# A relational graph layer: key one-hots by 16-bit pairs, source one-hots in three comparisons, additions set between other work

## The reference

```python
def _L0_gnn_ref(feat, weight, src, dst, etypes):
    h_src = feat[src]
    msg = jnp.zeros((h_src.shape[0], weight.shape[2]), dtype=feat.dtype)
    for r in range(num_rels):
        mask = etypes == r
        msg = msg + h_src * mask[:, None].astype(feat.dtype) @ weight[r]
    return jax.ops.segment_sum(msg, dst, num_segments=feat.shape[0])
h = jnp.maximum(_layernorm(x, axis=-1), 0.0)
x = x + _L0_gnn_ref(h, L0_gnn_weight, src, dst, edge_type_16)
```

## Time and profile before

| | |
|---|---|
| median of three | 1113.21 us |
| the profiled execution | 1110.19 us |
| its span, first to last instruction | 1108.4 us |
| TensorE (PE) busy | 958.2 us, 86% |
| VectorE (DVE) busy | 910.3 us, 82% |
| GpSimd (POOL) busy | 807.5 us, 73% |
| ScalarE (ACT) busy | 530.7 us, 48% |
| granted TensorE clock, mean | 0.966 |

### The profile page before, as it was taken

One profiled execution on the slowest core, in us unless ns is written; L12 is line 12 of the kernel. 1 busy time (PEld: TensorE's weight loads), 2 busy tenths in 40 slices (PEclk: granted clock), 3 DMA queues, 4 the chain that ended last, 5 costly groups with the idle time before them and its releaser, 6 DMA issues.

```text
span 1108.4 us, 57958 instructions
## 1 busy us (share of the span) xinstructions
PE 958.2 (86%) x24205; PEld 809.6 (73%) x24205; DVE 910.3 (82%) x3137; ACT 530.7 (48%) x1548; POOL 807.5 (73%) x644
## 2 busy tenths in 40 slices
PE   3999988899988888988899888989799798888996
PEld 1445777788877777877788777778687687776885
DVE  7755889898888689887899887998788689886884
ACT  4886454454445345544444453544344345444441
POOL 3231888888888888888787887878888888887760
PEclk9998999999999899998999998999999999998998
DMA  6697322222322222222232222232222222221312
GB/s 183 259 391 287 81 69 63 64 64 75 82 65 66 63 64 65 64 66 64 67 85 66 65 63 66 63 85 67 64 66 64 64 65 65 68 82 45 87 44 61
DMA packets 42713, 98.10 MB, mean 89 GB/s; under 512 B 14749, under 2 KB 14751, under 8 KB 42452
## 3 DMA queue, kind: packets, MB, share of 16 engines
q1 hardware_dynamic: 14870, 45.60, 12.3%
q0 software_dynamic: 19616, 20.13, 10.7%
q10 hardware_dynamic: 7966, 28.64, 6.7%
HBM read 66.69 MB, written 27.62 MB: 85 GB/s over the span
## 4 chain that ended last, share of the span: by engine, by line
PE 42%; DVE 26%; issue 12%; ACT 7%; POOL 7%; DMA 5%; DVEq 2%; ACTq 1%; POOLq 0%
PE ps L1288 15%; PE ps L1305 13%; DVE u L964 9%; POOL u L532 6%; DVE u L954 4%; PE ps L1329 4%; ACT u L605 3%; DMA u<-table,row_idx 3%; PE ps L1343 3%; DVE spreadv L872 2%; DVE accT L980 2%; ACT u L691 2%; DMA table<-u 2%; DVE rank L834 2%; PE ps L1210 1%
## 5 line engine op out<-in xcount | busy, mean ns | idle before, releaser
L532 POOL DMA_INDIRECT u<-table,row_idx x575 | 740.8, 1288 | 210.7 <-issue 140.5
L674 ACT CAST u<-ps 128x384 bf16<-128x384 f32 (+1 forms) x684 | 294.5, 465 | 443.5 <-PE ps L1288 433.3
L1288 PE MATMUL ps<-parts,u 128*128 128x192 bf16 x3724 | 356.2, 250 | 0.7 <-ACT key_p L595 0.5
L1288 PEld LDWEIGHTS ps<-parts,u 128*128 128x128 bf16 x3724 | 308.8, 99 | 11.5 <-issue 7.8
L1305 PE MATMUL ps<-u 32*64 32x272 bf16 (+1 forms) x15808 | 297.2, 279 | 8.4 <-issue 8.2
L964 DVE TENSOR_SCALAR u<-iota_key,z_sb 128x272 bf16<-128x272 f16 x1292 | 280.9, 286 | 8.8 <-DVE win_x L862 6.9
L1305 PEld LDWEIGHTS ps<-u 32*64 32x64 bf16 x15808 | 227.4, 105 | 49.7 <-issue 31.8
L954 DVE TENSOR_SCALAR u<-u,node_id 128x1152 bf16<-128x1152 f16 (+1 forms) x456 | 197.0, 487 | 0.0
L691 ACT COPY u<-ps 128x272 f32<-128x272 f32 (+3 forms) x304 | 102.0, 421 | 60.8 <-PE ps L1305 60.8
L980 DVE TENSOR_TENSOR accT<-accT,u 128x17 f32 (+1 forms) x392 | 71.3, 182 | 65.0 <-DVE accT L980 26.2
L1329 PE MATMUL ps<-u,w_cat 128*64 128x136 f32 x1216 | 90.4, 289 | 6.7 <-issue 5.2
(11 more groups left out here) (134 smaller groups left out, 769.9 us busy)
## 6 DMA issues: line engine op xcount, KB each, us to landing
u<-rel_dram SPq DMA_DIRECT2D x76, 544.0 KB
table<-u ACTq DMA_DIRECT2D x24, 1024.0 KB, 5.2
u<-table,row_idx POOLq DMA_INDIRECT x575
rel_dram<-rel_row SPq DMA_DIRECT2D x76, 4.2 KB
x_sb<-x SPq DMA_DIRECT2D x2, 448.0 KB
out<-h_sb SPq DMA_DIRECT2D x3, 224.0 KB
out<-h_sb ACTq DMA_DIRECT2D x3, 224.0 KB
msg_x<-table,spill_row POOLq DMA_INDIRECT x38
```

The lines of the kernel that those rows point to most:

```text
L532: pool.indirect_dma_start(out=msg_p[:, b, j, :], out_offset=None, in_=table, in_offset=bass.IndirectOffsetOnAxis(ap=row_idx[:, j, m:m + 1] ...
L674: act.copy(msg_s[:, u % MB, 0:width, :].rearrange("p q c -> p (q c)"), ps[gather_bank(u)][:, 0:width * ROW]).then_inc(s_gev, 1)
L1288: last = pe.matmul(there, hot[:, part % HRING, t - q * SK, at * P:(at + 1) * P], parts[:, t, :], start=t == blocks[0], stop=t == blocks[-1])
```

## The change

- **Key one-hots.** `z_sb` becomes 16-bit, and ACT writes each value twice, side by side. `key_hots` now makes a whole chunk, 6, 6 or 5 ranges, in one comparison of two tensors, `iota_key` against the pairs: 1632, 1632 or 1360 elements instead of 272. The ring `khot` has six chunks (two pairs of supers) as before.
- **Source one-hots.** Three comparisons for the whole pair (2176, 2048 and 2048 elements) instead of six. The ring `hot` has two whole pairs instead of three halves.
- **Slots and spills.** `placed` compares tensors of 16-bit pairs as well, for which the ranks are copied to pairs first (`rank2`). Spilled edges are ranked, placed and permuted once per two pairs ("two quads" of targets) instead of once per pair. `sort_turn` is a 16-bit matmul. All sorting steps use 128 partitions instead of 104, so GpSimd's prologue fills the other rows of `vals`.
- **Order.** `add_sums` is a generator, and the main loop of VectorE takes one addition from it after each of its larger steps. On TensorE the permutation goes from the end of chunk 0 to the middle of chunk 1, the turn from chunk 1 to chunk 2, and the batches of gathered rows are all summed in chunk 1. The planner's model has new costs for these.

```diff
-    KR, HCH, GB, MB = 34, ((0, 9), (9, SQ)), -(-SQ // 2), 9
-    HPART, HRING = max(high - low for low, high in HCH), 3
+    KR, HRING, GB, MB = 6, 2, -(-SQ // 2), 9
...
-    sum_at = (1, 1, 2, 2)
+    sum_at = (1, 1, 1, 1)
     def sort_pair(n, c, ahead, at):
         return n + ahead if n + ahead < NPR and c == at else None
-    permuted = lambda n, c: sort_pair(n, c, 2, 0)
-    turned = lambda n, c: sort_pair(n, c, 2, 1)
-    spilled = lambda n, c: sort_pair(n, c, 2, 2)
+    permuted = lambda n, c: sort_pair(n, c, 2, 1)
+    turned = lambda n, c: sort_pair(n, c, 2, 2)
     ranked = lambda n, c: sort_pair(n, c, 3, 2)
+    def spill_ranked(n, c):
+        return (n + 1) // 2 if c == 2 and n % 2 == 1 and n + 2 < NPR else None
+    def spill_placed(n, c):
+        return n // 2 if c == 0 and n % 2 == 0 else None
...
+            pool.tensor_copy(ident16[:, :], ident[:, :]).then_inc(s_const, 1)
+            pool.memset(z_sb[:, :, :], 0.0).then_inc(s_const, 1)
+            pool.wait_ge(s_const, 12)
+            pool.memset(vals[96:P, :, :, :], -1.0).then_inc(s_const, 1)
+            pool.wait_ge(s_const, 13)
             pool.memset(vals[:, :, 0:HJ, 4:5], 0.0).then_inc(s_const, 1)
             pool.memset(vals[:, :, HJ:SJ, 4:5], float(SW)).then_inc(s_const, 1)
-            pool.wait_ge(s_const, 10)
+            pool.wait_ge(s_const, 15)
...
-            def placed(hots, a, j, first, ranks, n):
-                there = hots[0:TP, :, :].rearrange("p j (a z) -> p a j z", a=a)
-                places = iota_slot[0:TP, first:first + n].rearrange("p (a j z) -> p a j z", a=1, j=1).to_broadcast([TP, a, j, n])
-                mine = ranks.rearrange("p (a j z) -> p a j z", j=j, z=1).to_broadcast([TP, a, j, n])
+            def placed(hots, first, ranks, tiles, n):
+                there = hots.rearrange("p t (h o) -> p t h o", o=2)
+                places = iota_slot[:, first:first + n].rearrange("p (t h o) -> p t h o", t=1, o=2).to_broadcast([P, tiles, n // 2, 2])
+                mine = ranks.rearrange("p t (h o) -> p t h o", h=1).to_broadcast([P, tiles, n // 2, 2])
                 return dve.tensor_tensor(there, places, mine, ALU.is_equal)
             def sort_slots(g):
                 dve.wait_ge(s_ranked, g + 1)
                 dve.wait_ge(s_ranges, g + 1)
-                step(dve.tensor_tensor(ranks[0:TP, :, :], ps[6][0:TP, 0:PT * SQ].rearrange("p (c q) -> p c q", q=SQ), ranges[0:TP, :, :],
-                                       ALU.mult))
-                step(dve.tensor_reduce(rank[0:TP, :], ranks[0:TP, :, :], AX, ALU.add))
+                dve.tensor_tensor(ranks[:, :, :], ps[6][:, 0:PT * SQ].rearrange("p (c q) -> p c q", q=SQ), ranges[:, :, :],
+                                  ALU.mult).then_inc(s_rread, 1)
+                dve.wait_ge(s_rread, g + 1)
+                step(dve.tensor_reduce(rank[:, :], ranks[:, :, :], AX, ALU.add))
+                by_tile = rank[:, :].rearrange("p (a j o) -> p a j o", j=HJ, o=1).to_broadcast([P, WINS, HJ, 2])
+                step(dve.tensor_copy(rank2[:, :, :].rearrange("p (j a) o -> p a j o", a=WINS), by_tile))
                 if g >= 1:
                     dve.wait_ge(s_z, g)
-                    dve.wait_ge(s_srank, g)
-                placed(slot_hot, WINS, HJ, 0, rank[0:TP, :], CAP).then_inc(s_slots, 1)
-                dve.tensor_scalar(spill_mask[0:TP, :], rank[0:TP, :], float(CAP), None, ALU.is_ge).then_inc(s_mask, 1)
+                placed(slot_hot, 0, rank2[:, :, :], PT, CAP).then_inc(s_slots, 1)
+                if g >= 2:
+                    dve.wait_ge(s_srank, g // 2)
+                dve.tensor_scalar(spill_mask[:, g % 2, :], rank[:, :], float(CAP), None, ALU.is_ge).then_inc(s_mask, 1)
...
-            def source_hots(n, c):
-                b, part, (low, high) = n % BCR, len(HCH) * n + c, HCH[c]
-                dve.wait_ge(s_bc[b], 16 * (n // BCR + 1))
-                if part >= HRING:
-                    last_n, last_c = divmod(part - HRING, len(HCH))
-                    dve.wait_ge(s_gat, GB * last_n + -(-HCH[last_c][1] // 2))
-                for k in range(SK):
-                    there = min(high, (NT - k + SK - 1) // SK)
-                    last = dve.tensor_scalar(hot[:, part % HRING, k, 0:(there - low) * P], bc[:, b, low * P:there * P],
-                                             node_id[:, k:k + 1], None, ALU.is_equal)
-                last.then_inc(s_hot, 1)
-            def key_hots(n, low, high):
+            def source_hots(n, k):
+                there = min(SQ, (NT - k + SK - 1) // SK)
+                if k == 0:
+                    dve.wait_ge(s_bc[n % BCR], 16 * (n // BCR + 1))
+                    if n >= HRING:
+                        dve.wait_ge(s_gat, GB * (n - HRING + 1))
+                last = dve.tensor_scalar(hot[:, n % HRING, k, 0:there * P], bc[:, n % BCR, 0:there * P], node_id[:, k:k + 1], None,
+                                         ALU.is_equal)
+                if k == SK - 1:
+                    last.then_inc(s_hot, 1)
+            def key_hots(n, c):
+                own, part = ranges_of(n, c), n * len(CHUNKS) + c
                 dve.wait_ge(s_zev, WINS * (n + 1))
-                for q in range(low, high):
-                    v = n * SQ + q
-                    if v >= KR:
-                        dve.wait_ge(s_agg, v - KR + 1)
-                    dve.tensor_scalar(khot[:, v % KR, :], iota_key[:, :], z_sb[:, n % 3, 1, q:q + 1], None, ALU.is_equal).then_inc(s_khot, 1)
+                if part >= KR:
+                    dve.wait_ge(s_agg, (n - KR // len(CHUNKS)) * SQ + own[-1] + 1)
+                there = khot[:, part % KR, 0:len(own), :].rearrange("p q (h o) -> p q h o", o=2)
+                keys = iota_key[:, :].rearrange("p (q h o) -> p q h o", q=1, o=2).to_broadcast([P, len(own), KEYS // 2, 2])
+                mine = z_sb[:, n % 3, 2 * (SQ + own[0]):2 * (SQ + own[-1] + 1)].rearrange("p (q h o) -> p q h o", h=1, o=2)
+                dve.tensor_tensor(there, keys, mine.to_broadcast([P, len(own), KEYS // 2, 2]), ALU.is_equal).then_inc(s_khot, 1)
...
                 added[0] += 1
+                yield
...
             for n in range(NPR):
                 ahead, sorting = n + 1 < NPR, n + 2 < NPR
+                adds = add_sums(n - 2) if n >= 2 else iter(())
                 if sorting:
                     sort_slots(n + 2)
                     sort_values(n + 2)
+                    next(adds, None)
                     if n + 3 < NPR:
                         sort_ranges(n + 3)
+                        next(adds, None)
                 if ahead:
-                    source_hots(n + 1, 0)
-                if n >= 2:
-                    add_sums(n - 2)
+                    for k in range(SK):
+                        source_hots(n + 1, k)
+                        next(adds, None)
+                    key_hots(n + 1, 0)
+                    next(adds, None)
+                if n % 2 == 0:
+                    spilled_rows(n // 2)
                 if ahead:
-                    key_hots(n + 1, KEYS_AT[0], KEYS_AT[1])
-                if sorting:
-                    sort_spilled(n + 2)
-                if ahead:
-                    source_hots(n + 1, 1)
+                    key_hots(n + 1, 1)
+                    next(adds, None)
                 for m in sums_in[n + 1] if ahead else ():
                     gathered_hots(m)
+                    next(adds, None)
                 if ahead:
-                    key_hots(n + 1, KEYS_AT[1], KEYS_AT[2])
-                if n % 2 == 1 and n + 2 < NPR:
-                    spilled_rows((n + 1) // 2)
-                if ahead:
-                    key_hots(n + 1, KEYS_AT[2], KEYS_AT[3])
+                    key_hots(n + 1, 2)
+                for _ in adds:
+                    pass
...
                 last_supers(n)
+                if n % 2 == 1 and sorting:
+                    sort_spilled((n + 1) // 2)
...
             def sort_turn(g):
                 pe.wait_ge(s_zev, WINS * (g + 1))
-                pe.transpose(ps[6][0:SQ, 0:P], z_sb[:, g % 3, 0, :], ident[:, :]).then_inc(s_relT, 1)
+                pe.matmul(ps[6][:, 0:P], z_sb[:, g % 3, 0:2 * P:2], ident16[:, :], start=True, stop=True).then_inc(s_relT, 1)
...
                 gather(n, c)
+                if permuted(n, c):
+                    sort_permute(permuted(n, c))
+                if spill_ranked(n, c) is not None:
+                    rank_spilled(spill_ranked(n, c))
                 if turned(n, c):
-                    rank_spilled(turned(n, c))
                     sort_turn(turned(n, c))
-                if spilled(n, c):
-                    permute_spilled(spilled(n, c))
+                if i:
+                    sum_sorted(*STREAM[i - 1])
+                if spill_placed(n, c) is not None:
+                    permute_spilled(spill_placed(n, c))
                 if c == 2 and n in TURNS_AT:
                     turn_last(TURNS_AT.index(n))
-                if i:
```

(3 more changed lines are left out.)

217 lines of the change are left out of this document (113 added, 104 removed).

## The result

| | before | after |
|---|---|---|
| median | 1112.58 us (1110.47 to 1114.58, 4 runs) | 1023.99 us (1020.55 to 1027.62, 4 runs) |
| span of the profiled execution | 1108.4 us | 1025.9 us |
| fetches: first start, last start | 106.13, 1078.54 us | 112.35, 993.80 us |
| fetches: total, held over 0.945 us each | 784, 205 us | 694, 114 us |

The ratio is 0.9204, with a 95% interval of 0.9167 to 0.9242.

The account below looks back on a forecast made before the run. It took GpSimd's fetch queue, held by VectorE, as the bound: 1110.2 us profiled plus 68 us more held time (76 pairs x 0.9) gives 1178, stated as 1180 us because the median is 3 us higher; 8-in-10 range 1065 to 1275 us.

Parts of the forecast that it names:

- The bound: GpSimd's queue of 613 fetches, never idle in 968 us: 763 us own work, 205 us held by VectorE.
- VectorE's terms: VectorE's time per pair: sources 2.02 us, keys 2.65, slots 0.34; in all about 1.9 us less per pair, 145 us.
- the ratio of 0.53: Held 2.7 of 5.09 us holding time per pair; the same ratio on 6.78 us gives 3.6 us, 68 us more overall.
- the low bound: Low side of the held-time term: additions might open each run in every even pair, about 1130 us.
- Has room: Spread of source row numbers, some 5 us later with the turn; its reader, 9 us behind, was said to have room.
- The start: GpSimd's prologue gets a memset of 6080 elements and small ones: taken as 0 us, upper end 8 us.
- Keys that hold nothing: Rival: new two-input key comparisons on VectorE hold no fetch; 38 us won, 1072 us, chance 0.17.
- Starved by long runs: Rival: back-to-back VectorE comparisons in odd pairs keep fetches waiting, 1240 to 1270 us, chance 0.20.
- No doubled rate: Rival: 16-bit pairs don't double VectorE's rate, keys take 5.05 us per pair; about 1297 us, chance 0.08.
- GpSimd no bound: Rival: GpSimd only looks like the bound; TensorE without 65 and 29 us waits and 35 us work, 981 us, chance 0.04.
- The signs named beforehand: Profile after: mean fetch about 1400 ns from 1288, gathered-row wait over 100 us, spread-value wait below 20, VectorE near 65%.

Follow-up runs that it names:

- g3: Kernel after with half the TensorE sums of ranges 1 to 15 left out, keys by 17 one-input comparisons per pair instead of three two-input: 1026.91 us.
- g4: Kernel after with half the TensorE sums of ranges 1 to 15 left out, source comparisons cut from three into six per pair: 1039.33 us.
- e4: Kernel after, all additions of a pair in one run behind the source comparisons: 1355.4 us, ratio 0.974, where before took 1380 to 1394 us.
- e3: Kernel before, one key comparison of 272 behind each source comparison: 1427.3 us, ratio 1.030, where before otherwise took 1380 to 1394 us.
- i1: Complete kernel after, 17 single key comparisons per pair and the turn of source numbers at the end of chunk 1's sums: 975.18 us, ratio 0.881.

## Why the prediction was wrong, point by point

- **The bound was right, and after it was not alone.** GpSimd's queue has no idle time before or after, and the result is the change of its held time less 6 us of later start (90 - 6, against 82.5 us measured). That the queue alone would hold the time up is not shown by taking held time away: in g3 that gained nothing, as the second bound stood there.
- **VectorE's terms were right.** Sources forecast 2.02 us, measured 2.02 (718.40 to 720.42). Keys 2.65, measured 0.925 x 2 + 0.783 = 2.63 us, so the pairs do double the rate. Slots 0.34, measured 0.35. Its busy time fell by 143.5 us, forecast 145. TensorE's fell by 58 us, forecast 35.
- **The failing step is the ratio of 0.53**, held time to the time of all instructions that can hold, carried from before to after. By kind, from the table and the time per kind (76 pairs): sources 130 of 183 us, 0.71, before, and 22 of 154 us, 0.14, after; keys 76 of 200 us, 0.38. With 0.53 for all, 3.6 us per pair were forecast; 1.5 came, so that 68 us more became 90 us less. For the keys the forecast step was too high, but in the right direction (2.65 x 0.53 = 1.4 us, measured 1.0). For slots and spills 48 us became 4: they take less time, and the source run that 21 fetches waited through behind them no longer keeps a fetch. The sign was lost on the sources. A ratio for each kind would not have saved the forecast: 0.71 of 154 us is 109 us for the sources, and with the 76 us of the keys 185 us or more would have been held, 20 us less than before at most and not 90.
- **I had seen the cue.** The rows showed that a fetch is let go only at the end of a run, and the low bound even had additions opening the runs. But I took the hold to be the nature of a source comparison, wherever it stands. It is not. Take the ends of source comparisons with another directly behind at which a fetch was waiting, and count those after which it was done within 1 us: 28 of 265 before, 38 of 38 after, 54 of 54 with halves (g4). The trace of before had a hint: 13 of the 14 fetches that met the second of three comparisons were let in at its end, while the 95 that met the first all waited to the end of the run or beyond.
- **Why the sources hold so much less stays open.** Their length gives 11 of 108 us (g4). Additions between are not it (e4), and a key comparison between does not end the hold at once (e3). What else differs (the steps ahead of them, 128 instead of 104 partitions, the places of the buffers) was not tried apart.
- **"Has room" was wrong.** The later turn costs VectorE 74.7 us of waits. It hid behind the queue, and became the second bound at the same 1025 us.
- **The start was costed at 0, with 8 us as its end;** it is 6 us. The fill itself hides, but it holds VectorE's first steps (2.5 and 3.2 us longer), and the first fetch is late with them.
- **The rivals.** Keys that hold nothing: wrong, though its 1072 us was nearer. Starved by long runs: it exists, 15 times, 34 us. No doubled rate: wrong. GpSimd no bound, 981 us: wrong for before and after. That i1, with queue and loop both loosened, came to 975 us, near that figure, is luck: the 981 us were added up from other waits.
- **The signs named beforehand** were read as said: mean fetch 1125 ns, not 1400; TensorE's wait for gathered rows 30.0 us, not over 100; its wait for the spread values gone, as forecast; a key comparison of 1632 lasts 0.92 us and the fetches caught in one end 0.82 us after a comparison's end, as forecast; VectorE's share 75%, not near 65.

## What to carry to other kernels

Where one engine's queue never pauses, add up its own work and what it is held for by kind of holder. A share of held time belongs to the order in which it was measured: here it fell from 0.71 to 0.14 for the same source elements, cut and placed otherwise, so give it a wide range when the order changes, or measure it in the new order first. When a large saving in the bound's queue gains nothing, as in g3, look for the first wait that has grown; here two bounds stood within a few us, and both edits together moved the time (1024 to 975 us), where the single keys alone did not; the turn alone was not seen. A fill on GpSimd is not free because GpSimd idles later; see whom it holds.
